# Normed tokens of the slot mixer made inside the fourth attention of a gated transformer stack, with another order of VectorE's norms there

## The reference

```python
x = x + tanh(g_xattn[3]) * L3_xattn(layernorm(x), ctx)   # norms both again inside; 1 head, 256 wide
x = x + tanh(g_ffn[3]) * L3_ffn(layernorm(x))

def L3_ffn(x, ...):                       # x: (16, 100, 256), already normed
    h = gelu(concat(x, mean(slots)) @ w1 + b1)
    logits = (h @ w2 + b2) / (abs(tau) + 0.1)
    alpha = softmax over the top 8 of 64 slots
    si = einsum('bts,btd->bsd', alpha, x) / (alpha.sum(axis=1) + 1e-8)
    ...                                   # a GRU step on the slots, attention among slots, norm
    return einsum('bts,bsd->btd', alpha, slot_values) @ wo + bo
```

## Time and profile before

| | us |
|---|---|
| median of 3 runs | 1812.4 |
| the three runs | 1812.17, 1812.4, 1819.4 |
| profiled execution | 1815.32 |
| its span | 1813.5 |

### The profile page before, as it was taken

One profiled execution on the slowest core, in us unless ns is written; L12 is line 12 of the kernel. 1 busy time (PEld: TensorE's weight loads), 2 busy tenths in 40 slices (PEclk: granted clock), 3 DMA queues, 4 the chain that ended last, 5 costly groups with the idle time before them and its releaser, 6 DMA issues.

```text
span 1813.5 us, 30878 instructions
## 1 busy us (share of the span) xinstructions
PE 1622.6 (89%) x9150; PEld 1154.0 (64%) x9150; DVE 971.4 (54%) x3169; ACT 627.5 (35%) x1780; POOL 318.5 (18%) x434
## 2 busy tenths in 40 slices
PE   6898889859999899999999899799998997777787
PEld 2555555659999766666666567577776446665555
DVE  4778787532222244444444435555554667774664
ACT  3545455412333233333333233133331004443232
POOL 4555555220000210000000000100000112122000
PEclk8999999869999999999999899899998999998797
DMA  4000005149999510000000000100000001210000
GB/s 108 15 17 20 20 19 151 58 165 330 312 322 323 178 30 14 12 12 6 12 12 6 1 7 18 32 20 24 18 18 7 23 26 45 88 43 1 1 18 19
DMA packets 86297, 115.80 MB, mean 64 GB/s; under 512 B 16610, under 2 KB 77762, under 8 KB 81090
## 3 DMA queue, kind: packets, MB, share of 16 engines
q1 hardware_dynamic: 82722, 110.43, 19.2%
q0 software_dynamic: 2432, 4.34, 0.8%
q10 hardware_dynamic: 1056, 0.01, 0.0%
HBM read 104.51 MB, written 6.95 MB: 61 GB/s over the span
## 4 chain that ended last, share of the span: by engine, by line
PE 71%; issue 10%; DVE 7%; ACT 4%; DMA 3%; POOL 2%; SPq 1%; ACTq 1%; DVEq 0%; POOLq 0%
PE bank L2294 14%; PE bank L2407 8%; PE bank L2590 6%; PE bank L2380 5%; PE bank L2683 5%; PE bank L2353 5%; PE bank L2391 4%; PE bank L2437 4%; PE bank L2604 3%; PE bank L2636 3%; PE bank L2345 3%; PE bank L2652 2%; PE bank L2770 2%; DMA work<-in_F_b1c 2%; DVE work L1547 1%
## 5 line engine op out<-in xcount | busy, mean ns | idle before, releaser
L1053 ACT ACTIVATE work<-bank,work 100x361 f32<-100x361 f32 (+1 forms) x272 | 159.0, 591 | 256.2 <-DVE work L1547 235.4
L2407 PEld LDWEIGHTS bank<-work 128*100 128x100 f32 x1760 | 183.6, 170 | 58.5 <-issue 31.4
L1556 DVE COPY work<-bank 128x300 f32<-128x300 f32 (+1 forms) x272 | 123.1, 489 | 174.8 <-PE bank L2391 174.0
L2407 PE MATMUL bank<-work 128*100 128x64 f32 (+1 forms) x1760 | 187.0, 257 | 14.9 <-DVE work L1556 14.8
L2590 PE MATMUL bank<-work 128*128 128x128 f32 x1216 | 143.0, 275 | 2.7 <-DMA work<-in_F_b1c 2.7
L1547 DVE TENSOR_REDUCE work<-bank 100x1 f32<-100x361 f32 x208 | 101.9, 528 | 77.5 <-PE bank L2380 66.5
L2590 PEld LDWEIGHTS bank<-work 128*128 128x128 f32 x1216 | 140.6, 192 | 4.4 <-ACT work L1185 1.9
L1899 DVE SCALAR_TENSOR_TENSOR work<-bank,work 128x128 f32<-128x128 f32 x160 | 56.1, 351 | 161.3 <-PE bank L2590 147.0
L2380 PE MATMUL bank<-work 64*100 64x361 f32 (+1 forms) x512 | 119.4, 544 | 1.1 <-ACT work L1038 0.6
L811 POOL TENSOR_TENSOR work<-work,neg_half 100x1 f32<-100x1 f32 x96 | 52.8, 550 | 373.0 <-DVE work L1503 372.3
L2294 PE MATMUL bank<-L_WkvT,work 96*128 96x512 f32 x192 | 98.2, 637 | 15.6 <-ACT work L1014 14.7
(11 more groups left out here) (313 smaller groups left out, 2866.8 us busy)
## 6 DMA issues: line engine op xcount, KB each, us to landing
work<-in_F_w SPq DMA_DIRECT2D x58, 1024.0 KB, 5.7
work<-in_ctxT SPq DMA_DIRECT2D x64, 135.4 KB, 2.2
work<-in_ctx SPq DMA_DIRECT2D x32, 192.0 KB, 2.5
work<-in_F_b SPq DMA_DIRECT2D x20, 128.0 KB, 6.5
work<-sorted_x SPq DMA_DIRECT2D x20, 128.0 KB, 2.8
sorted_y<-work SPq DMA_DIRECT2D x20, 128.0 KB, 6.1
work<-in_ctx SPq DMA_DIRECT2D x32, 78.8 KB, 2.4
F_weight<-in_F_w SPq DMA_DIRECT2D x2, 1024.0 KB, 6.5
```

What stands on the lines that cost most here:

```text
L1053: nc.scalar.activation(pr[:, 0:NK], S_bank[k][0:T, 0:NK], ACT.Exp, bias=nmax[k][0:T, :], accum_out=rsum[j][0:T, h:h + 1]).then_inc(s.exped ...
L1556: nc.vector.tensor_copy(PT[k][:, 0:CH, :], PT_bank[k][:, 0:CH * T].rearrange("p (c t) -> p c t", c=CH)).then_inc(s.probs_copied.sem, 1)
L2407: ins = nc.tensor.matmul(to, PT[k][:, c, :], values, start=(c == 0), stop=(c == CH - 1))
```

## The change

Inside the fourth attention, the mixer's norm of x is now made as in the second and third: residual(t − 1) copies the turned tokens of t − 2 out of R_bank (into SXT), aggregates the statistics and writes variance + eps; GpSimd makes the power after x's second one; mixture_norm writes GN; project(t) turns it. New here is that GpSimd copies GN into XS, where the weighted sums read it, and that mixture_norm waits until the copy before has read GN. Batch 15's tokens are normed, turned and copied at the start of the mixer, between the first and the second hidden group. The aggregates, the powers of 16, the norms, tokens_turn and ScalarE's copies leave the mixer. XS, SXT and two of the four pairs' buffers lie elsewhere in SBUF.

VectorE's order in a batch of the fourth attention is a new function, fourth_attend: the copy of the turned probabilities and residual(t − 1) come right after x's first statistics; x's first norm and the second statistics follow; then o_scale, x's second norm, and the mixer's norm of t − 1.

```diff
+            def mixture_tokens(L, t):
+                mixture_rstd(L, t)
+                if L == 3:
+                    wait_count(pool, mx3.ln_x, 3 * (t + 1))
+                    nc.gpsimd.tensor_copy(XS[0:T, bass.ds(t, 1), 0:D], GN[0:T, :].rearrange("p (o d) -> p o d", o=1)
+                                          ).then_inc(mx3.bo_added, 1)
...
-                elif L == 3:
-                    with pool.Fori(0, B // 2 - 1) as i:
-                        for j in range(2):
-                            norms(2 * i + j + 2, j)
...
             def mixture_norm(L, t):
                 s = mixture[L]
                 wait_count(dve, s.rstd_x, t + 1)
+                if L == 3:
+                    wait_count(dve, s.bo_added, t)
...
-                    if L in (1, 2) and not (isinstance(t, int) and t == 0):
+                    if L > 0 and not (isinstance(t, int) and t == 0):
                         mixture_keep(L, t - 1, R_bank)
...
-                    stats = Rst6[0:T, :] if L < 3 else x_st6[0:T, bass.ds(t, 1), :].rearrange("p o n -> p (o n)")
-                    nc.vector.bn_stats(stats, xt).then_inc(s.x_stats.sem, 1)
+                    nc.vector.bn_stats(Rst6[0:T, :], xt).then_inc(s.x_stats.sem, 1)
...
-                    if L in (1, 2):
+                    if L > 0:
                         mixture_stats(L, t)
...
+                def fourth_attend(t, j, more):
+                    two_more = two_follow(t, more)
+                    started = not (isinstance(t, int) and t == 0)
+                    maximum(t, j, 0)
+                    if more:
+                        wait_for(dve, s.pv, t)
+                        ln_ctx_norm(t + 1, 1 - j)
+                    if two_more:
+                        ln_ctx_stats(t + 2, j)
+                        ln_x(t + 2, j, 0)
+                    probs_copy(t, j, 0)
+                    if started:
+                        residual(t - 1, 1 - j)
+                    if two_more:
+                        ln_x_norm(t + 2, j, 0)
+                        ln_x(t + 2, j, 1)
+                    o_scale(t, j)
+                    if two_more:
+                        ln_x_norm(t + 2, j, 1)
+                    if started:
+                        mixture_norm(L, t - 1)
...
             def slot_mixer():          # VectorE
-                wait_for(dve, at[3].x_stats, B)
-                for t in range(B):
-                    nc.vector.bn_aggr(Fmv[0:T, t, :], x_st6[0:T, t, :]).then_inc(s.ln_x, 1)
-                dve.wait_ge(s.ln_x, B)
-                nc.vector.tensor_scalar(Frs[0:T, :], Fmv[0:T, :, 1], LN_EPS, None, ALU.add).then_inc(s.ln_x, 1)
+                mixture_norm(3, B - 1)
...
-                dve.wait_ge(s.rstd_x, 1)
-                for t in range(B):
-                    nc.vector.tensor_scalar(XS[0:T, t, 0:D], X[0:T, t, :], Fmv[0:T, t, 0:1], Frs[0:T, t:t + 1],
-                                            ALU.subtract, ALU.mult).then_inc(s.ln_x, 1)
+                dve.wait_ge(s.x_turned, 1)
+                mixture_keep(3, B - 1, bank[0])
...
                     dve.wait_ge(s.out, u + 1)
-                    dve.wait_ge(s.bo_added, u + 1)
+                    dve.wait_ge(s.bo_added, B + u + 1)
...
-                    if L in (1, 2) and not (isinstance(t, int) and t == 0):
+                    if L > 0 and not (isinstance(t, int) and t == 0):
                         ins = mixture_turn(L, t - 1, R_bank)
...
-                for u in range(4):
-                    tokens_turn(u)
                 hidden(0)
-                for u in range(4, 6):
-                    tokens_turn(u)
+                mixture_turn(3, B - 1, bank[0]).then_inc(s.x_turned, 1)
                 hidden(1)
                 slot_logits(0)
-                for u in range(6, 8):
-                    tokens_turn(u)
                 hidden(2)
...
                     pe.wait_ge(s.alpha, 3 * (u + 1))
+                    pe.wait_ge(s.bo_added, 2 * (u + 1))
```

More of the change, by code:

```diff
@@ L357, in flamingo_kernel @@
                       "out resid")
+        mixture = {1: mx1, 2: mx2, 3: mx3}
         area = Area()
@@ L438, in flamingo_kernel @@
         B1_first = area.take(2 * HID0 // P)
-        Fmv, Frs = area.take(B, 2), area.take(B)
         area.at = attention_end
@@ L456, in flamingo_kernel @@
         area.at = 0
-        XS = area.take(B, D + 1)
         MEAN = area.take(2, 1)
@@ L463, in flamingo_kernel @@
         pairs_at = area.at
-        SXT = area.take(2, NTOK)
         HG = area.take(NTOK)
@@ L492, in pair_buffers @@
             return w
-        pair = [pair_buffers(k) for k in range(SLOTS_AT_ONCE)]
-        assert area.at >= unused_by_3 and area.at >= pairs_at + 3 * NTOK
+        pair = [pair_buffers(k) for k in range(2)]
+        assert pairs_at + NTOK <= unused_by_3 and area.at <= unused_by_3
+        area.at = unused_by_3
+        XS = area.take(B, D + 1)
         SI, SIT = area.take(D), area.take(2, P)
@@ L503, in flamingo_kernel @@
         TAU = area.take(2)
+        late_at = area.at
+        SXT = area.take(2, NTOK)
+        assert area.at <= attention_end + 2 * NTOK
+        area.at = late_at
+        pair += [pair_buffers(k) for k in range(2, SLOTS_AT_ONCE)]
+        assert area.at <= attention_end + 2 * NTOK
         slot_loads = []
@@ L882, in attention @@
                             norms(2 * i + j + 2, j)
-                            mixture_rstd(L, 2 * i + j - 1)
-                    mixture_rstd(L, B - 3)
-                    mixture_rstd(L, B - 2)
+                            mixture_tokens(L, 2 * i + j - 1)
+                    mixture_tokens(L, B - 3)
+                    mixture_tokens(L, B - 2)
                 end(pool)
-            def rstd_x(s, p, last=True):
-                begin(pool, p)
-                pool.wait_ge(s.ln_x, B + 1)
-                nc.gpsimd.tensor_tensor(Frs[0:T, :], Frs[0:T, :], neg_half[0:T, 0:B], ALU.pow).then_inc(s.rstd_x, 1)
-                if last:
-                    end(pool)
             def routed_experts():
@@ L935, in slot_mixer @@
                 s = mx3
-                rstd_x(s, 7, last=False)
+                begin(pool, 7)
+                mixture_tokens(3, B - 1)
                 pool.wait_ge(s.bo_scaled, 1)
-                pool.wait_ge(s.ln_x, 2 * B + 1)
                 for u in range(B // 2):
@@ L1237, in gelu @@
                                          ).then_inc(s.gelu, 1)
-                for u in range(B // 2):
-                    act.wait_ge(s.x_turned, u + 1)
-                    nc.scalar.copy(SXT[:, :, 2 * T * u:2 * T * (u + 1)].rearrange("p c (m t) -> p m c t", m=2),
-                                   bank[u % 2][:, 0:4 * T].rearrange("p (m c t) -> p m c t", m=2, c=2)).then_inc(s.x_copied, 1)
-                    if u in (3, 5):
-                        gelu((u - 3) // 2)
-                gelu(2)
-                gelu(3)
+                for g in range(B // 4):
+                    gelu(g)
                 def weights(u, k):
@@ L1663, in attend @@
                         maximum(t, j, 1)
-                    if L == 3 and more:
-                        wait_for(dve, s.pv, t)
-                        ln_ctx_norm(t + 1, 1 - j)
                     if two_more:
@@ L1670, in attend @@
                     started = not (isinstance(t, int) and t == 0)
-                    if PAIRS[L] == 0:
-                        for h in range(H):
-                            probs_copy(t, j, h)
-                            if h + 2 < H:
-                                maximum(t, j, h + 2)
-                            if h == 0 and started:
-                                residual(t - 1, 1 - j)
                     for p in range(PAIRS[L]):
@@ L2719, in slot_mixer @@
                 ins.then_inc(s.const_sums, 1)
-                def tokens_turn(u):
-                    wait_count(pe, s.x_copied, u - 1)
-                    pe.wait_ge(s.ln_x, B + 1 + 2 * u + 2)
-                    for m in range(2):
-                        for c in range(2):
-                            ins = tr(bank[u % 2][:, (2 * m + c) * T:(2 * m + c + 1) * T],
-                                     XS[0:T, 2 * u + m, c * P:(c + 1) * P], ident[0:T, 0:T])
-                    ins.then_inc(s.x_turned, 1)
                 def hidden(g):
-                    pe.wait_ge(s.x_copied, 2 * (g + 1))
+                    pe.wait_ge(s.x_copied, 4 * (g + 1))
                     if g >= 2:
```

8 lines of the change are left out of this document (3 added, 5 removed).

## The result

The changed kernel takes 1799.44 us (median of 4 runs, 1796.23 to 1801.82), the kernel before 1813.79 in the same comparison (1812.17 to 1819.4). The ratio is 0.9914, 95% interval [0.9892, 0.9936]: faster. Forecast were 1805.3 us and a gain of 7.1; the measured gain is 14.35. A second comparison later gave 1801.56 against 1814.97, ratio 0.9930 [0.9902, 0.9959].

The account below looks back on a forecast made before the run. It took the fourth attention's batch (9.83 us) to be bound by a ring in which TensorE waits for VectorE's late copy. Attention 0.8 plus mixer's front 6.3 gave 7.1 us off the 1812.4 median: 1805.3 us, range 1799 to 1812.

Parts of the forecast that it names:

- The period of a batch: Fourth attention: a batch takes 9.6 us instead of 9.83, so 14 batches gain 3.2 us.
- VectorE's ring: Fourth attention, VectorE's chain per batch: 9.22 us, 9.41 with the wait for GpSimd's power, 9.58 with the longer context norms.
- The best case of 9.4: Fourth attention: a batch of 9.4 us, if GpSimd's copy does not delay the context's norms.
- TensorE's ring: Fourth attention, TensorE's chain per batch: 9.83 less the 0.69 wait plus 0.26 for two transposes, 9.40 us.
- GpSimd's copy beside the norms: Fourth attention: GpSimd's added copy into XS takes 0.55 us and makes the context's norms 0.17 us late.
- The tail: End of the fourth attention, last batches without norms ahead: added steps and transposes lose 2.4 us.
- The mixer's front: Slot mixer's start to first logits on VectorE: 12.0 us instead of 18.4, gain taken as 6.3, bounds 3.5 and 7.
- Behind the first logits: Slot mixer after the first logits: the same VectorE chain, 7.97 us to the sums, moves as it is.
- Rival A: Fourth attention: rings run free with a short GpSimd copy, 9.4 us a batch; 9.8 us gained, 1802.6 us; chance 0.30.
- B: Mixer's front gains only 3.5 us at half clock, a batch takes 9.75 us; 2.2 gained, 1810.2 us; chance 0.13.
- C: Fourth attention: late output scaling delays the next turn of the output, batch 10.5 us; 5.5 slower, 1817.9 us; chance 0.07.

Follow-up runs that it names:

- e4: The changed kernel with one more VectorE copy of the turned tokens, to an unused place, in each fourth-attention batch; 1813.4 us in one execution.
- e1: The kernel before with VectorE's new order in the fourth attention alone, the mixer's tokens made as before; 1801.01 us, ratio 0.9937.
- e9: The kernel of e5 with TensorE's two transposes of the mixer's norm issued twice; 1800.24 us in one execution.
- e5: The changed kernel with the copy of the normed tokens into XS taken from GpSimd and given to ScalarE; 1796.22 us, ratio 0.9913.
- e6: The changed kernel with three to eight cheap TensorE products at each of five places at the fourth attention's end and ahead of the mixer; 1793.85 us, ratio 0.9907.
- e7: The changed kernel with the edits of e5 and e6 plus five 512-column products between the mixer's last logits and first sums; 1789.68 us, ratio 0.9864.
- e8: The changed kernel once more, unaltered, compared with the kernel before; 1801.56 us, ratio 0.9930.
- e2: The changed kernel with VectorE's old order in the fourth attention, norms ahead of the copy of the probabilities; 1818.03 us, ratio 1.0028.
- e3: The changed kernel with TensorE's two transposes of the mixer's norm issued twice in the fourth attention; 1804.35 us in one execution.
- e10: The kernel of e5 with one more VectorE copy of the turned norms, to a place nobody reads; 1797.89 us in one execution.

## Why the forecast was wrong, step by step

**The period of a batch, the step that failed.** The forecast's 9.6 us stood on VectorE's ring, and e4 shows that VectorE's ring does set the batch of the changed kernel: the mechanism was right and the size was not, 9.58 against 9.19. The best case of 9.4 stood on TensorE's ring, and this was too long as well, 9.40 against 9.10. With TensorE at 9.40 even a right sum for VectorE could not have brought the forecast below 9.4.

**TensorE's ring.** The forecast put it at 9.83 − 0.69 + 0.26 = 9.40 us. It is 9.10: the wait was worth 0.92, not 0.69 (e1: 8.91), and the two transposes cost 0.17 to 0.19, not 0.26 (e9). The number for the wait was read from the list of waits of matmuls. From start to start it is 0.84, and 0.08 more hung on the step behind it. The Trainium skill (page Perfetto Trace Analysis, section Tensor Engine Instruction) warns of this: the profiler estimates the end of a TensorE instruction from its size instead of observing it. The trace agrees: the next group starts 0.17 us before that end (1591.49 + 0.93 = 1592.42, and 1592.25).

**VectorE's ring.** Forecast 9.22, with the wait for GpSimd's power 9.41, with the longer norms 9.58. Measured 9.03 in the short half and 9.35 in the long one. In the short half the distances from the maximum through the copies to X's small sum held: 3.77 against 3.81, then 0.39, 0.33, 0.85, 0.53, 0.22, of which the first was taken as 0.38 and the others as they are. Too large were places where the next instruction doesn't need the one before: small sum to x's norm 0.10 (taken 0.20) and to the reciprocal 0.07 (0.20). The mixer's norm to the maximum was 0.33 (0.44), but 0.52 in every second batch, so that term came out right on the mean. The mixer's norm does wait for GpSimd: the power ends at 1585.72 (1585.18 + 0.54) and the norm starts at 1585.76, 0.51 behind x's second norm where the forecast had 0.44 and a wait of 0.19 (0.16 by its own terms). GpSimd's second power starts 0.50 us behind the first (1584.68 and 1585.18), not 0.65. One error had the other sign: the scaling to the second norm took 0.53, taken as 0.45. Together they make a batch 0.39 us too long, and 14 batches multiply it.

**GpSimd's copy beside the norms.** Forecast 0.55 us and 0.17 on the norms. Measured 0.40 or 0.62 us, and 0 or 0.19 on the norms, in turn. The mechanism and the size held for one batch in two, and in e5 it is gone. The Trainium skill (page SBUF — State Buffer, section SBUF: two separate sides) calls this an exclusive lock of the port pair that VectorE and GpSimd share: the trace agrees for the norms in the long half (1.14 us) and, more plainly, for e6's compare of 1.41 us beside GpSimd's sums. It does not show why the copy, which started first, grew to 0.62 us as well. In the short half GpSimd's copy started 0.37 us ahead of the norms and ended 0.03 into them (1586.76 against 1586.73), in the long half only 0.18 ahead.

With the mean of 9.19 the 15 distances between the maxima gave 7.6 us instead of 3.2. This is 4.4 of the 9.5 us that the profiled execution gained beyond the forecast. It would have been more, but the first distance took 10.93 us and 10.14 before. It is 9.5 to 9.6 in e4 to e7 and e9 and 10.9 to 11.1 in the other executions: TensorE worked at the granted clock 0.50 there for longer or shorter, and e6 and e8, which are alike up to there, differ in it.

**The tail.** Forecast +2.4, measured +4.0. The added steps cost less than forecast (0.7 by e6, 1.5 by e1); the rest is the granted clock, which the forecast held at full until the last project step. It was 0.50 from 1635 us on, 14 us ahead of the mixer; before, it stayed at 1.00 until some 5 us ahead of it. In e1, without the tokens, it was 0.53 in 1630 to 1635, so it isn't the tokens. Why the kernel before kept its clock through most of batch 15 isn't settled: TensorE had idle times of 0.56 to 0.85 us there as well.

**The mixer's front.** Forecast 12.0 us to the first logits, measured 11.3 (e2: 12.2). Right in mechanism, and 0.7 us too long in size. The clock did return to 1.00 within the products with the weights and stayed there, as taken. The same front took 11.2 (e5) to 12.7 us (e3) in the experiments without products added ahead of it. Nothing in this step failed.

**Behind the first logits** the forecast had no change, and 2.3 us went, nearly all behind the first sums. The steps there are the same. The clock is granted in other stretches than before, and from the first sums to the last sum into X it is 127.3 us before, 125.1 and 125.2 after, and 124.3 to 126.9 in the experiments; e1, with the mixer of before, has the 126.9. That it is the clock was not tested by itself, and this share stays open.

**The start,** 3.6 us, was scatter (e8).

**The rivals.** Rival A, the rings run free, came nearest, and it went further than A had it: 9.19 a batch instead of 9.4, and 1799.4 instead of 1802.6 us. It had 0.30. Its mechanism held in part: the copy was short (0.40) in one batch of two, and the batch was VectorE's and not TensorE's. B and C did not occur. C's ring over the scaling of the output (L1561) stood close by: the turn of the output started 0.04 us late in the long half, and 0.23 to 0.31 late once VectorE had 0.27 us more to do (e4, e10). The range of 1799 to 1812 held the time at its very edge, and by luck: its lower end was said to be A with a full front, and this gives 1801.9 by the forecast's own terms (1802.6 less 0.7). The bound of the period, 9.41 from below, was too high.

## What to carry to other kernels

Take what a removed wait is worth from start to start of the two groups around it, not from the idle column behind a pipelined matmul: the row of the weight load shows it better. Take the mean of all kinds of batches, and look whether the step behind the wait gets shorter too. On an engine that works without gaps, measure the distance of independent neighbours and of dependent ones apart, and sum with the right one; an error of 0.1 us at three places becomes 4 us over 14 batches. Where two rings of two engines come out alike, an addition to either shows in full (e9, e10), so I would expect little from shortening one alone; this was not tried. Look at the last batches of a pipeline apart: here they lost the clock. And in a loop whose body holds two batches look at both, for they need not take the same time.

## What the runs showed of the hardware

- TensorE's granted clock fell to 0.50 in a tail with waits of 0.56 to 0.84 us between products, and cheap products into a bank that nobody read at the time kept it at 1.00: 3.3 us in the tail and 1.5 in the mixer's front (e6), 2.7 in the sums (6.44 to 3.75, e7).
- A copy of 100x256 on GpSimd takes 0.40 us, and 0.62 where it starts 0.18 us ahead of three VectorE norms, which then take 1.14 instead of 0.95.
- VectorE's maximum starts 0.52 us behind the instruction ahead of it when it is the first of the loop's body after a jump back, and 0.33 otherwise, in the changed kernel, e3, e4, e5, e9 and e10 alike.
- One VectorE compare of 100x256 beside GpSimd's last sum of 100x512 took 1.41 us instead of 0.43, and ended 0.28 behind that sum.
- The first maximum of the fourth attention, up to which the work of all these kernels is the same, lies anywhere from 1488.0 (e10) to 1500.7 us (e4) in the profiles. A term of a few us is to be read within a stage, not from a span.
